# A GRU recurrence on one core: six 256-column matmuls on constant operands in each step that has no input products

## The chip, the cores and the metric

The kernel runs on one core of a Trainium2 chip. The metric is the device time of one execution in microseconds (us). TensorE (PE in the profile, PEld for its weight loads) does the matmuls, VectorE (DVE), ScalarE (ACT) and GpSimd (POOL) the element-wise work, SyncE (SP) issues DMAs. TensorE's clock has two levels here, 2.4 GHz (written 1.00 in the profile) and 1.2 GHz (0.50).

## The reference

Four layers run one after the other on x of shape (8, 256, 512), each added to its input: a masked attention over channels, a modulated attention over tokens, a GRU over the 256 tokens, and an attention over eight block sums with a layer norm. The change lies in the GRU. Cut to what matters:

```python
def cell(h, x):
    gi = x @ W_ih + b_ih
    gh = h @ W_hh + b_hh
    i_r, i_z, i_n = jnp.split(gi, 3, axis=-1)
    h_r, h_z, h_n = jnp.split(gh, 3, axis=-1)
    r = jax.nn.sigmoid(i_r + h_r)
    z = jax.nn.sigmoid(i_z + h_z)
    n = jnp.tanh(i_n + r * h_n)
    h_new = (1.0 - z) * n + z * h
    return (h_new, h_new)
x = x + scan(cell, cond, x)        # 256 steps, batch 8, width 512
```

## The kernel before, in words

The first two layers (`attention`) take the first 1137 us, the recurrence the stretch from 1139 to 2028 us, the last layer (`block_attention`) the rest.

**A step of the recurrence.** Each engine walks the same list of 256 steps, held together by semaphores. The state is kept as two float16 parts (high and low), each weight too. On TensorE, `gate` (L1252) issues matmuls of 16 columns (8 batch rows, high and low part) with a new 128x128 weight load before each; a step has 96 of them, for the gates r (into `pA`), n (`pB`) and z (`pC`). The order is written out by hand: 32 of them (16 for r, 8 for z, 8 for n) need the first half of the state alone and stand behind the first of these waits, the other 64 behind the second:

```python
pe.wait_ge(lo_done, step * 2 + 1)
...
pe.wait_ge(lo_done, step * 2 + 2)
```

Between, VectorE sums the halves (L1447, L1451), ScalarE takes sigmoid and tanh (L1356) and writes the next step's starting values into the banks (`seed`, L1347), VectorE forms the new state (L1492) and splits off its low part (L1497), which releases TensorE for the next step (`lo_done`). GpSimd adds the state to x and copies the next step's input term (L1535, once per step).

**Blocks of steps.** `blocks` (L1203) cuts the 256 steps into 8 blocks of 32. In each of the first seven, 8 plain steps come first (`begins` true), then 24 product steps, which also compute the input products for the next block: eight matmuls of 256 columns per step (`products`, L1244), issued after the step's own 96, into bank 0 of `pD`. In every second plain step of these blocks GpSimd splits x for the next block into float16 parts (`split`, L1529 and L1531). The last block has 32 plain steps, without products and without a split. So 88 steps are plain: 7 times 8, and 32.

`pG[1]`, bank 1 of `pD`, is used by the products ahead of the recurrence only. `w_in` holds the split input weights and isn't written during the recurrence.

Of the kernel before, what the change touches and what calls it, by code (L numbers as in the profile page):

```python
# [14 lines left out]
P = 128  # L15

B, N, D = 8, 256, 512
# [3 lines left out]
NC, DC = N // P, D // P  # L21
# [3 lines left out]
TB = N // NB  # L25
# [1114 lines left out]
def recurrence(nc, sem, sb, W_ih, W_hh, b_ih, b_hh, Wk3, Wo3, pA, pB, pC, pD, xT, ident, condT, rep, w_ih, woT, block_sums,  # L1140
               norm, norm_from):

    with ExitStack() as ctx:  # L1143
# [3 lines left out]
        w_in, wi_lo = [w_ih[0][:, n, :, :] for n in range(2)], w_ih[3]  # L1147
# [45 lines left out]
        pG = [pD[:, 0, 0:B * TB], pD[:, 1, 0:B * TB]]  # L1193
# [9 lines left out]
        def blocks(eng, step, split, product):  # L1203


            with eng.Fori(0, BLOCKS - 1) as blk:
                with eng.Fori(0, PLAIN // BODY) as k:
                    for j in range(BODY):
                        step(blk * TB + k * BODY + j, j, blk, True)
                        if j == 0:  # L1210
                            split(blk + 1, k)
                with eng.Fori(0, RZ) as m:
                    for j in range(BODY):
                        step(blk * TB + m * BODY + (PLAIN + j), j, blk)
                        product(blk + 1, m, j, False)
                with eng.Fori(RZ, MC) as m:
                    for j in range(BODY):
                        step(blk * TB + m * BODY + (PLAIN + j), j, blk)
                        product(blk + 1, m, j, True)
            with eng.Fori(0, TB // BODY) as k:  # L1220
                for j in range(BODY):
                    step(k * BODY + (N - TB + j), j, BLOCKS - 1, True)

        @block.sync
        def _(sp):
            sp.dma_start(bih_c[:, :], b_ih.rearrange("(c p) -> p c", p=P), allow_slow_non_contiguous=True).then_inc(b_ld, 16)
            sp.dma_start(bhh_c[:, :], b_hh.rearrange("(c p) -> p c", p=P), allow_slow_non_contiguous=True).then_inc(b_ld, 16)
            sp.dma_start(staged, W_hh.rearrange("(c p) n -> p c n", p=P)).then_inc(w_ld, 16)
            for tile, w in ((wk, Wk3), (wo, Wo3)):
                sp.dma_start(tile, w.rearrange("(c p) n -> p c n", p=P)).then_inc(wko_ld, 16)  # L1230

            *columns, gamma_bc, norm_ld = norm
            cond, rms_w, beta, gamma = norm_from
            for tile, row in zip(columns, (cond[1:2, :].rearrange("a n -> (a n)"), rms_w, beta)):
                sp.dma_start(tile[:, :], row.rearrange("(c p) -> p c", p=P), allow_slow_non_contiguous=True).then_inc(norm_ld, 16)
            sp.dma_start(gamma_bc[:, :], gamma.rearrange("(a n) -> a n", a=1).broadcast_to([P, D])).then_inc(norm_ld, 16)

        @block.tensor
        def _(pe):
            def products(m, k, bank):  # L1240

                for w in range(2):
                    for part in range(2):
                        last = nc.tensor.matmul(bank, w_in[w][:, k, bass.ts(m, P)], x_part[:, part, k, :, :].rearrange("p b t -> p (b t)"),  # L1244
                                                start=(k == 0 and w == 0 and part == 0), stop=(k == DC - 1 and w == 1 and part == 1))
                return last

            def step(step, j, blk, begins=False):

                pe.wait_ge(seeded, step * 6 + 4)  # L1250

                def gate(ps, first, part, ks):  # L1252
                    for c in CHUNKS[part]:
                        o = (c - CHUNKS[part][0]) * 2 * B
                        for k in ks:
                            for w in w_part:
                                last = nc.tensor.matmul(ps[part][:, o:o + 2 * B], w[:, k, (first + c) * P:(first + c) * P + P],  # L1257
                                                        moving[j % 2][:, k, :, :].rearrange("p s b -> p (s b)"), start=False,
                                                        stop=(k == DC - 1), skip_group_check=True)
                    return last  # L1260


                R, Z, N_ = 0, DC, 2 * DC
                K_A, K_B = CHUNKS
                pe.wait_ge(lo_done, step * 2 + 1)
                gate(pR, R, 1, K_A)
                gate(pR, R, 0, K_A)
                gate(pZ, Z, 0, K_A)
                gate(pN, N_, 0, K_A)
                pe.wait_ge(lo_done, step * 2 + 2)  # L1270
                gate(pR, R, 0, K_B).then_inc(r_ps, 1)
                gate(pZ, Z, 0, K_B).then_inc(z_ps, 1)
                gate(pN, N_, 0, K_B).then_inc(n_ps, 1)
                gate(pR, R, 1, K_B).then_inc(r_ps, 1)
                pe.wait_ge(seeded, step * 6 + 6)
                gate(pN, N_, 1, K_B)
                gate(pN, N_, 1, K_A).then_inc(n_ps, 1)
                gate(pZ, Z, 1, K_A)
                gate(pZ, Z, 1, K_B).then_inc(z_ps, 1)

            def nothing(*_):
                pass

            def product(blk, m, j, is_n):
                if j == 0:
                    pe.wait_ge(x_lo, blk * DC + DC)
                    pe.wait_ge(gi_out, blk * MC + m)
                for k in range(j * DC // BODY, (j + 1) * DC // BODY):
                    last = products(m, k, pG[0])
                if j == BODY - 1:  # L1290
                    last.then_inc(gi_ps, 1)


            def first_products(m):
                if m >= 2:
                    pe.wait_ge(gi_out, m - 1)
                for k in range(DC):
                    if m == 0:
                        pe.wait_ge(x_lo, k + 1)
                    last = products(m, k, pG[m % 2])  # L1300
                last.then_inc(gi_ps, 1)


            def transpose(n):
                w, bank = ((wk, pA), (wk, pB), (wo, pC), (wo, pA))[n]
                if n == 3:
                    pe.wait_ge(wT_ok, 1)
                for hf in range(2):
                    kc = 2 * (n % 2) + hf
                    for hc in range(DC):  # L1310
                        last = nc.tensor.transpose(bank[:, hf, hc * P:hc * P + P], w[:, kc, hc * P:hc * P + P], ident[:, :])
                last.then_inc(wT_ps, 1)

            pe.wait_ge(wi_lo, DC)
            for m in range(RZ):
                first_products(m)
            pe.wait_ge(wko_ld, 32)
            for n in range(MC - RZ):
                transpose(n)
                first_products(RZ + n)  # L1320
            pe.wait_ge(wT_ok, 4)

            pe.wait_ge(w_lo, DC)
            pe.wait_ge(lo_done, 2)
            for ps in (pR, pN, pZ):
                for part in range(2):
                    last = nc.tensor.matmul(ps[part], w_part[0][:, 0, 0:P], moving[0][:, SLICE[part], :, :].rearrange("p c s b -> p (c s b)"),
                                            start=True, stop=True)
            last.then_inc(begun, 1)
            blocks(pe, step, nothing, product)  # L1330

        @block.scalar
        def _(act):
# [38 lines left out]
            def nothing(*_):  # L1372
                pass
# [35 lines left out]
        def _(dve):  # L1409
# [108 lines left out]
            def nothing(*_):  # L1518
                pass
# [322 lines left out]
```

## Time and profile before

| | us |
|---|---|
| median of 3 runs (lowest, highest) | 2088.25 (2083.18, 2089.26) |
| the profiled execution | 2086.28 |
| span of its trace, first to last instruction | 2084.4 |
| TensorE busy | 1862.4 (89%) |
| VectorE busy | 1268.6 (61%) |
| ScalarE busy | 1117.4 (54%) |
| GpSimd busy | 376.8 (18%) |
| TensorE's mean granted clock | 0.878 |

Busy time is the time in which an engine had an instruction running. For TensorE it counts each matmul to its modelled end, so a row of 16-column matmuls that overlap shows about 0.17 us each and what a run of matmuls takes is read from the starts of its rows. "idle before" in square brackets is the time in which the engine had nothing running ahead of that row, with the instruction whose result ended the wait.

### The profile page before, as it was taken

What the parts mean: (1) busy time and instruction counts of PE and PEld (TensorE: products, weight loads), DVE (VectorE), ACT (ScalarE), POOL (GpSimd) and SP (SyncE); (2) the same over time, 40 slices, a digit from 0 to 9 for tenths busy, and PEclk for the clock granted to TensorE, in tenths of its full rate; (3) what the DMA queues carried; (4) which work ended last, traced back from release to release, by engine and by line L of the source; (5) the groups of instructions that cost most, each with busy time, mean ns of one, the idle gap of its engine ahead of it and who ended that gap; (6) DMA issues with size and microseconds to landing.
All of it is one profiled execution on the core that took longest, in us unless ns stands there. A gap on an engine that the chain in (4) does not pass through costs nothing. (4 is left out here: it accounts for less than half of the span.)

```text
span 2084.4 us, 86393 instructions
## 1 busy us (share of the span) xinstructions
PE 1862.4 (89%) x32542; PEld 1372.1 (66%) x32542; DVE 1268.6 (61%) x5543; ACT 1117.4 (54%) x4105; POOL 376.8 (18%) x1398
## 2 busy tenths in 40 slices
PE   7877998999989999999978998989898999999876
PEld 4234364454635546355557898989898989889775
DVE  6454483645736366374143777777777777777766
ACT  0342636546364463636553565656565666666554
POOL 3000000000000000000000333333334333333335
PEclk7788999999999999999998697969697988989556
DMA  5122203132041321302123000000000000000002
GB/s 190 70 66 71 68 21 106 53 76 83 9 110 42 82 78 35 95 15 74 69 61 107 1 1 0 0 0 0 0 0 0 0 0 0 0 0 0 0 0 81
DMA packets 103527, 86.76 MB, mean 42 GB/s; under 512 B 15616, under 2 KB 90496, under 8 KB 103440
## 3 DMA queue, kind: packets, MB, share of 16 engines
q1 hardware_dynamic: 101392, 84.38, 14.0%
q8 instruction: 59, 0.97, 0.2%
q10 hardware_dynamic: 1664, 1.18, 0.2%
q14 instruction: 28, 0.23, 0.0%
q0 software_dynamic: 384, 0.01, 0.0%
HBM read 60.20 MB, written 21.00 MB: 39 GB/s over the span
## 5 line engine op out<-in xcount | busy, mean ns | idle before, releaser
L1257 PE MATMUL bank_pair_A<-moving,rep 128*128 128x16 f16 x8192 | 328.4, 172 | 67.2 <-DVE moving L1497 64.1
L1257 PEld LDWEIGHTS bank_pair_A<-moving,rep 128*128 128x128 f16 x8192 | 268.4, 99 | 96.4 <-DVE moving L1497 81.2
L1257 PE MATMUL bank_pair_B<-moving,rep 128*128 128x16 f16 x8192 | 321.3, 171 | 0.0
L1257 PE MATMUL bank_pair_C<-moving,rep 128*128 128x16 f16 x8192 | 321.3, 171 | 0.0
L1356 ACT ACTIVATE r_gate<-r_pre 128x16 f32<-128x16 f32 x512 | 110.5, 216 | 305.6 <-DVE r_pre L1447 305.6
L1257 PEld LDWEIGHTS bank_pair_C<-moving,rep 128*128 128x128 f16 x8192 | 265.8, 99 | 0.0
L1257 PEld LDWEIGHTS bank_pair_B<-moving,rep 128*128 128x128 f16 x8192 | 265.8, 99 | 0.0
L1244 PE MATMUL bank_pair_D<-x_part,w_in 128*128 128x256 f16 x1536 | 211.5, 286 | 5.8 <-ACT gi_rz L1383 3.3
L1137 POOL TENSOR_TENSOR x<-x,w_in 128x512 f32<-128x512 f32 x8 | 10.2, 1274 | 962.5 <-DMA w_in<-w_in 962.5
L1447 DVE TENSOR_REDUCE r_pre<-bank_pair_A 128x16 f32<-128x32 f32 x512 | 98.1, 192 | 137.5 <-PE bank_pair_A L1257 136.4
L834 ACT ACTIVATE probs<-bank_pair_A 128x1024 f32<-128x1024 f32 x128 | 131.0, 1024 | 90.5 <-PE bank_pair_A L598 90.1
L1043 DVE TENSOR_REDUCE head_max<-bank_pair_A 128x2 f32<-128x1024 f32 x128 | 155.7, 1216 | 36.3 <-PE bank_pair_A L579 36.2
L1043 DVE TENSOR_REDUCE head_max<-bank_pair_B 128x2 f32<-128x1024 f32 x128 | 155.4, 1214 | 13.9 <-PE bank_pair_B L579 13.9
L1244 PEld LDWEIGHTS bank_pair_D<-x_part,w_in 128*128 (+1 forms) x1536 | 143.5, 101 | 26.8 <-ACT gi_rz L1383 3.5
L1535 POOL COPY n_terms<-gi_n 128x32 f32 (+1 forms) x257 | 54.3, 211 | 530.1 <-DVE moving L1497 431.9
L610 PE MATMUL bank_pair_C<-probs,w_in 128*32 128x512 f32 x1024 | 139.7, 618 | 1.0 <-ACT probs L834 0.2
L834 ACT ACTIVATE probs<-bank_pair_B 128x1024 f32<-128x1024 f32 x128 | 130.8, 1022 | 16.3 <-PE bank_pair_B L598 16.3
L1356 ACT ACTIVATE z_gate<-z_pre 128x16 f32<-128x16 f32 x512 | 110.4, 216 | 25.0
L1456 DVE TENSOR_TENSOR n_terms<-bank_pair_B,r_gate 128x32 f32<-128x32 f32 x512 | 97.7, 191 | 38.0 <-ACT r_gate L1356 0.9
L598 PEld LDWEIGHTS bank_pair_A<-rep 128*128 128x128 f16 x512 | 41.2, 98 | 114.7 <-ACT probs L834 68.4
L885 ACT ACTIVATE sq<-bank_pair_C 128x256 f32<-128x256 f32 x48 | 18.4, 384 | 174.6 <-PE bank_pair_C L640 174.6
L1451 DVE TENSOR_REDUCE z_pre<-bank_pair_C 128x16 f32<-128x32 f32 x512 | 95.8, 187 | 20.6
(260 smaller groups left out, 3639.4 us busy)
## 6 DMA issues: line engine op xcount, KB each, us to landing
rep<-parts SPq DMA_DIRECT2D x256, 64.0 KB
parts<-parts SPq DMA_DIRECT2D x48, 256.0 KB, 2.1
q_rep<-parts SPq DMA_DIRECT2D x32, 256.0 KB, 4.7
k_rep<-parts SPq DMA_DIRECT2D x64, 128.0 KB, 2.8
w_in<-in_x_dram SPq DMA_DIRECT2D x8, 512.0 KB, 4.0
x<-in_x_dram SPq DMA_DIRECT2D x8, 512.0 KB, 4.3
parts<-parts SPq DMA_DIRECT2D x32, 128.0 KB, 2.5
out_dram<-res SPq DMA_DIRECT2D x16, 256.0 KB, 2.1
```

The costliest lines, as they stand in the source:

```text
L598: last = nc.tensor.matmul(pair[u % 2][:, j // 2, (j % 2) * N:(j % 2) * N + N], k_rep[:, h, kc * P:kc * P + P], q_rep[:, h, queries], start ...
L610: last = nc.tensor.matmul(pC[32 * j:32 * j + 32, g % 2, :], v_aug[:, kc, 4 * g + j, :], probs[w % 2][:, j, :], start=(kc == 0), stop=(kc = ...
L834: nc.scalar.activation(probs[u // 2 % 2][:, :, u % 2 * N:u % 2 * N + N], pair[u % 2][:, :, :].rearrange("p a (b t) -> p (a b) t", b=2), AC ...
L885: nc.scalar.activation(sq[m % 2][:, :], qk_bank[m % 3][:, 0:N], ACT.Square).then_inc(sq_ok, 1)
L1043: nc.vector.tensor_reduce(head_max[:, 2 * n:2 * n + 2], pair[n % 2][:, :, :], AX.X, ALU.max).then_inc(s_max, 1)
L1244: last = nc.tensor.matmul(bank, w_in[w][:, k, bass.ts(m, P)], x_part[:, part, k, :, :].rearrange("p b t -> p (b t)"), start=(k == 0 and w ...
L1257: last = nc.tensor.matmul(ps[part][:, o:o + 2 * B], w[:, k, (first + c) * P:(first + c) * P + P], moving[j % 2][:, k, :, :].rearrange("p s ...
L1356: nc.scalar.activation(dst[:, SLICE[part], :], src[:, SLICE[part], :], func, scale=1.0 / GS).then_inc(done, 1)
L1447: nc.vector.tensor_reduce(r_pre[:, SLICE[part], :], halves(pR[part]), AX.X, ALU.add).then_inc(r_sum, 1)
L1451: nc.vector.tensor_reduce(z_pre[:, SLICE[part], :], halves(pZ[part]), AX.X, ALU.add).then_inc(z_sum, 1)
L1456: nc.vector.tensor_tensor(n_terms[:, SLICE[part], 0:2, :], pN[part].rearrange("p (c s b) -> p c s b", s=2, b=B), r_gate[:, SLICE[part], :] ...
L1535: nc.gpsimd.tensor_copy(n_terms[:, :, 2, :], gi_n[:, bass.ds(step, 1), :, :].rearrange("p o c b -> p (o c) b")).then_inc(n_in, 1)
```

## The change

At the end of TensorE's part of a step, if the step is plain (`begins`), six matmuls follow. Their stationary operand is a 128x128 piece of the high part of `w_in`, their moving operand 256 columns of its low part, and they write bank 1 of `pD`. Nothing reads that bank before the last layer overwrites it, they carry no semaphore and wait for none. The 168 product steps, and all other engines, stay as they are. TensorE gets 88 times 6, that is 528 matmuls more, each with its weight load.

```diff
                 gate(pN, N_, 1, K_A).then_inc(n_ps, 1)
                 gate(pZ, Z, 1, K_A)
                 gate(pZ, Z, 1, K_B).then_inc(z_ps, 1)
+                if begins:
+                    for k in range(6):
+                        nc.tensor.matmul(pG[1], w_in[0][:, k % DC, 0:P], w_in[1][:, k % DC, 0:B * TB], start=True, stop=True)
 
             def nothing(*_):
                 pass
```

## Rows read from the trace of the kernel before

**Rows 1.** The page: TensorE's granted clock in 40 slices, in tenths

```profile
PEclk7788999999999999999998697969697988989556
```

**Rows 2.** Windows, TensorE alone: stretch, length, busy (matmuls), granted clock, DMA

```profile
1142.00:1170.00 28.00, 21.66 (x750) 0.50 0.01 2
1170.30:1182.30 12.00, 12.00 (x288) 0.50 0.01 1
1183.00:1251.00 68.00, 67.81 (x2100) 1.00 0.00 1
1258.00:1282.00 24.00, 18.46 (x643) 0.50 0.00 0
1282.60:1284.60 2.00, 2.00 (x26) 0.50 0.00 0
...
1923.50:2025.00 101.50, 83.16 (x2875) 0.50 0.00 0
```

**Rows 3.** Timeline of GpSimd, L1535 alone, one per step: start, length

```profile
1172.26 0.21 POOL L1535 COPY n_terms<-gi_n 128x32 f32 x1 [1.97 <-DVE moving L1497]
...
1185.04 0.21 POOL L1535 COPY n_terms<-gi_n 128x32 f32 x1 [2.86 <-DVE moving L1497]
1188.39 0.21 POOL L1535 COPY n_terms<-gi_n 128x32 f32 x1 [1.95 <-DVE moving L1497]
...
1198.37 0.21 POOL L1535 COPY n_terms<-gi_n 128x32 f32 x1 [1.92 <-DVE moving L1497]
...
1259.79 0.21 POOL L1535 COPY n_terms<-gi_n 128x32 f32 x1 [1.06 <-DVE moving L1497]
...
1266.92 0.21 POOL L1535 COPY n_terms<-gi_n 128x32 f32 x1 [1.07 <-DVE moving L1497]
...
1990.15 0.21 POOL L1535 COPY n_terms<-gi_n 128x32 f32 x1 [2.04 <-DVE moving L1497]
...
1996.93 0.21 POOL L1535 COPY n_terms<-gi_n 128x32 f32 x1 [2.04 <-DVE moving L1497]
```

**Rows 4.** Timeline of TensorE: end of a plain step, start of the next

```profile
1253.93 0.39 PE L1257 MATMUL bank_pair_C<-moving,rep 128*128 128x16 f16 x10
1255.07 0.56 PE L1257 MATMUL bank_pair_A<-moving,rep 128*128 128x16 f16 x16 [0.74 <-DVE moving L1497]
...
1258.82 0.59 PE L1257 MATMUL bank_pair_A<-moving,rep 128*128 128x16 f16 x16 [1.04 <-DVE moving L1497]
...
1260.98 0.57 PE L1257 MATMUL bank_pair_C<-moving,rep 128*128 128x16 f16 x16
1262.17 0.59 PE L1257 MATMUL bank_pair_A<-moving,rep 128*128 128x16 f16 x16 [0.61 <-DVE moving L1497]
```

**Rows 5.** Timeline: a split on GpSimd beside VectorE's low part of the state

```profile
1265.15 0.70 POOL L1531 TENSOR_TENSOR x_part<-xT,x_part  x1 [0.18 <-POOL x_part L1529]
1265.36 0.53 DVE L1497 TENSOR_TENSOR moving<-state,moving 128x16 f16<-128x16 f32 x1
```

**Rows 6.** Timeline of TensorE: products in two product steps

```profile
1174.77 1.87 PE L1244 MATMUL bank_pair_D<-x_part,w_in 128*128 128x256 f16 x8
1176.42 0.62 PE L1257 MATMUL bank_pair_A<-moving,rep 128*128 128x16 f16 x16
...
1206.54 1.03 PE L1244 MATMUL bank_pair_D<-x_part,w_in 128*128 128x256 f16 x8
1207.41 0.55 PE L1257 MATMUL bank_pair_A<-moving,rep 128*128 128x16 f16 x16
```

**Rows 7.** Windows, TensorE alone, columns as in rows 2: the attention, a block's end

```profile
1069.70:1073.10 3.40, 1.86 (x13) 1.00 0.00 0
...
1585.10:1588.50 3.40, 3.15 (x102) 1.00 0.00 0
1588.50:1591.90 3.40, 2.78 (x96) 0.50 0.00 0
```

**Rows 8.** Timeline of TensorE: the first matmuls of the last layer

```profile
2029.19 1.09 PE L1631 MATMUL bank_pair_B<-block_sums,rep 128*128 128x64 f32 x4 [3.37 <-PEq L1143]
```

## The prediction

> **What bounds the kernel now.** I read the page first: TensorE is busy for 89% of the span, but its granted clock dips again and again from 1137 us on, where the recurrence runs [rows 1]. Then the windows cut at the block borders show what the dips follow. In every one of the seven blocks the plain steps run at 0.50, the product steps reach 1.00 after a while and stay there, and the 32 plain steps of the last block run at 0.50 throughout [rows 2]. So the clock falls where a step is only its 96 small matmuls, and comes back once the eight products are added.
>
> What does a low clock cost? Step times are the distances between GpSimd's copies, one per step [rows 3]:
> - a product step at 0.50: (1185.04 - 1172.26) / 3 = 4.26 us;
> - a product step at 1.00: (1198.37 - 1188.39) / 3 = 3.33 us;
> - a pair of plain steps at 0.50 in blocks 0 to 6, one with a split: 1266.92 - 1259.79 = 7.13 us;
> - a plain step at 0.50 in the last block: (1996.93 - 1990.15) / 2 = 3.39 us.
>
> Only the first is bound by TensorE: it goes from the products straight into the next step. A plain step is bound by the chain state, matmuls, VectorE, ScalarE, state: TensorE waits 0.61 us for VectorE before it begins [rows 4]. A pair with a split is longer, by 7.13 - 2 x 3.39 = 0.35 us, because VectorE's low part is stretched to 0.53 us until GpSimd's split beside it ends [rows 5]; that has nothing to do with TensorE.
>
> So the low clock hurts in the product steps that still run at 0.50: of the seven stretches four last about 12 us (three steps) and three about 2 us (one step); rows 2 show one of each kind. That is 4 x 3 + 3 = 15 steps at 4.26 - 3.33 = 0.93 us, 14 us in all. In the last block it costs about 0.06 us a step.
>
> **The change, part by part.** Nothing is removed or moved. TensorE gets 528 matmuls of 256 columns with their weight loads; no queue, DMA or semaphore is added. They need no data of the step, so they start as soon as the last small matmul is issued, and the question is whether they are done when the new state is there. Behind them on TensorE stands the next step's first group, for which VectorE and then all others wait.
>
> *Price of one.* The products have the same shape [rows 6]: at 1.00 (1207.41 - 1206.54) / 8 = 0.109 us, at 0.50 (1176.42 - 1174.77) / 8 = 0.206 us. Six take 0.65 us or 1.24 us.
>
> *In a step at 1.00: hidden.* A small matmul's row is 0.17 us long, so ten in 0.39 us follow each other every 0.025 us and are issued until 1254.18; the next step starts at 1255.07 [rows 4]. Six added ones would be done by 1254.83, 0.24 us before. The step then costs what the chain costs, and the product steps at 1.00 show it: 3.33 us, with eight such matmuls on board. With a split 0.35 us come on top, so a pair takes 7.0 us.
>
> *In a step at 0.50: not hidden.* Sixteen in 0.57 us are 0.027 us apart and issued until 1261.41, the next step starts at 1262.17 [rows 4]; six more end at 1262.65, 0.48 us late. The step becomes bound by TensorE like a cold product step, two matmuls shorter: 4.26 - 2 x 0.206 = 3.85 us. A pair goes from 7.13 to 7.70 us, 0.29 us a step more; a step of the last block would go from 3.39 to 3.85 us, 0.46 us more. The split's cost disappears in it, since TensorE is later than VectorE.
>
> *Which steps are at which clock?* This decides. Per step TensorE streams 96 x 16 = 1536 columns in a plain step, 3584 in a product step, and 3072 in the new plain step: between what fell and what held. The nearest rows on the side that held are in the second attention, where TensorE did twelve to thirteen 256-column matmuls in 3.4 us, about 3072 columns, and was still at 1.00 after it. On the side that fell, the border of a block: at 1585 us the last product had just been issued, small matmuls followed, and 3.4 us later the clock was at 0.50 [rows 7]. A step of the last block at 3.33 us is as dense as the attention's stretch, so I let the clock **hold in the last block**. In blocks 0 to 6 a pair takes 7.0 us, its density is 5% lower, and the steps with a split have a long wait in them; I take it that the clock **falls there after a step or two**. Once at 0.50, can the added ones raise it? Cold product steps with eight needed up to three steps; six in 3.85 us are thinner in columns than eight in 4.26 us, so no: the block stays low until its products come, which then pay as before. Block 0 enters low [rows 2] and stays so for about 7 plain steps.
>
> *The sum.* Steps at 0.50: 7 in block 0 and 5.5 in each of six blocks, 40 in all, x 0.29 = +11.6 us. Last block 31 x 0.06 = -1.9 us. The cold product steps: still about 15, 0. The last layer: TensorE stands idle for 3.37 us before it [rows 8], so a clock held to the end brings it nothing, 0; the six after the last step lie in this idle time, 0. Together +9.7 us on the profiled execution's 2086.28, so 2096. That execution lay 2.0 us below the median, so against the 2088.25 us shown the forecast is **2098 us**, 0.5% slower.
>
> The Trainium skill, page "TensorE: Matmul & The Clock Gate", section "Why this matters for your kernels", speaks of something else than density: it asks that there be no long idle gaps between bursts of matmuls, and names them as what brings the clock down. This trace doesn't bear that out here: the clock fell with no wait of TensorE longer than about 1.04 us between plain steps [rows 4]. Taken at its word, it would have the clock up in all steps before and after, and the change at nothing; read as "shorter gaps hold the clock", it is the first rival.
>
> **The rivals.**
> 1. *The clock holds in all plain steps after block 0.* For it: the gaps at 1.00 shrink to some 0.24 us, and the new step is nearer the product step than the old plain one. Against: a split step adds 0.35 us of waiting, and the border row. The time: 12 of the 15 cold product steps go, -11.2 us; six blocks with three pairs at 7.0 instead of 7.13, -2.3 us; last block -1.9 us; block 0 +2.0 us. Sum -13.4 us, 2075 us. It ends on the faster side; it decides if one split step at 1.00 doesn't bring the clock down. 15%.
> 2. *It holds in some of the seven blocks.* Each block that holds changes the sum by -1.6 us for its 5.5 steps, -0.4 us for its pairs and -1.9 us for two cold product steps, about -3.9 us; with two to four of six the total is +2 to -6 us, 2082 to 2090 us. 18%.
> 3. *It falls in the last block too.* For it: a single fall is enough, since nothing in this block raises the clock again. Its 31 steps then cost 31 x 0.46 = +14.3 us instead of -1.9 us: 2098 + 16.2 = 2114 us. Against: the attention's row, the same columns in the same time. 12%.
>
> **How the numbers follow.** The forecast has 55%, its own range 2092 to 2103 us: the number of steps before the fall moves it by 0.29 us each (35 to 45 steps), cold product steps by 0.93 us each, where a few more or fewer are likely because the blocks' borders move against the clock's changes. A measurement of this kernel tells about 0.3% (6.3 us) from no change. Slower by more: nearly all of the forecast and of rival 3, 0.64. Faster by more: rival 1 and the edge of rival 2, 0.17. Between: the rest, 0.19. The range leaves out rival 1 and the last of rival 3: 2081 to 2114 us.
>
> **What would show it right or wrong.** The granted clock of plain steps: 0.50 for most of each plain stretch in blocks 0 to 6, with GpSimd's copies 3.85 us apart; 1.00 from 1920 us on to the end of the recurrence, with copies 3.33 us apart. In the windows from the first product of a block to 1.00, still 2 to 12 us. If copies are 3.85 us apart in the last block, rival 3 is right; if the product steps of blocks 1 to 6 are all at 3.33 us, rival 1. The forecast is wrong in kind if plain steps at 0.50 stay at 3.4 to 3.7 us (the matmuls would then be cheaper than the products), or if plain steps at 1.00 are longer than 3.4 us without a split.

## The result, and the profile after

The change made the kernel slower: 2107.56 us median of 4 executions (2106.87 to 2111.59) against 2088.03 us (2083.18 to 2089.26; one execution more than in the table ahead of the prediction), a ratio of the two times of 1.0098 with a 95% interval of 1.0078 to 1.0117, or +19.5 us. The forecast was +9.7 us. The sign, the mechanism and the price of a step were right; in one place, the last block, the clock did the opposite of what the forecast let it do.

The page of the kernel after, in the lines that answer to [rows 1]:

```profile
span 2109.7 us, 87449 instructions
...
PE 1951.9 (93%) x33070; PEld 1434.9 (68%) x33070; DVE 1270.7 (60%) x5543; ACT 1119.0 (53%) x4105; POOL 376.3 (18%) x1398
...
PE   7877998999999999999978999999999999999996
...
PEclk7788999999999999999997897969697979888556
```

TensorE is busy 89.5 us longer, and its mean granted clock is 0.875, as good as the 0.878 before: the added matmuls kept it working and did not keep its clock up. In windows cut at the clock's changes (length, TensorE's busy time and matmuls, granted clock, DMA share, GB/s), the plain stretches of blocks 0, 1 and 2, a part of block 2's cold product steps, and the last block:

```profile
1147.00:1173.00 26.00, 26.00 (x697) 0.50 0.00 1
...
1262.00:1289.00 27.00, 27.00 (x725) 0.50 0.00 0
1375.00:1401.00 26.00, 26.00 (x695) 0.50 0.00 0
1405.30:1408.70 3.40, 3.40 (x78) 0.50 0.00 0
1942.00:2046.00 104.00, 104.00 (x2757) 0.50 0.00 0
```

In [rows 2] the same stretches were at 0.50 with TensorE busy for 77% to 82% of them; now it is busy all the time, still at 0.50. GpSimd's copies, one per step, in a plain stretch of block 1 and in the last block:

```profile
1268.31 0.21 POOL L1538 COPY n_terms<-gi_n 128x32 f32 x1 [2.11 <-DVE moving L1500]
1272.48 0.21 POOL L1538 COPY n_terms<-gi_n 128x32 f32 x1 [1.57 <-DVE moving L1500]
1276.00 0.21 POOL L1538 COPY n_terms<-gi_n 128x32 f32 x1 [2.11 <-DVE moving L1500]
...
1993.49 0.21 POOL L1538 COPY n_terms<-gi_n 128x32 f32 x1 [2.36 <-DVE moving L1500]
...
2001.17 0.21 POOL L1538 COPY n_terms<-gi_n 128x32 f32 x1 [2.36 <-DVE moving L1500]
```

A cold pair with a split takes 1276.00 - 1268.31 = 7.69 us (7.13 before, [rows 3]; forecast 7.70), a cold step of the last block (2001.17 - 1993.49) / 2 = 3.84 us (3.39 before; forecast 3.85). TensorE's timeline at the start of the last block shows the moment at which the clock falls, and what it costs:

```profile
1932.72 0.36 PE L1257 MATMUL bank_pair_A<-moving,rep 128*128 128x16 f16 x8
...
1934.34 0.81 PE L1282 MATMUL bank_pair_D<-w_in 128*128 128x256 f16 x6
1935.31 0.56 PE L1257 MATMUL bank_pair_A<-moving,rep 128*128 128x16 f16 x16 [0.15 <-DVE moving L1500]
1935.72 0.34 PE L1257 MATMUL bank_pair_C<-moving,rep 128*128 128x16 f16 x8
1935.92 0.34 PE L1257 MATMUL bank_pair_B<-moving,rep 128*128 128x16 f16 x8
1936.36 0.36 PE L1257 MATMUL bank_pair_A<-moving,rep 128*128 128x16 f16 x8
...
1937.57 0.56 PE L1257 MATMUL bank_pair_C<-moving,rep 128*128 128x16 f16 x16
1937.99 1.44 PE L1282 MATMUL bank_pair_D<-w_in 128*128 128x256 f16 x6
1939.22 0.62 PE L1257 MATMUL bank_pair_A<-moving,rep 128*128 128x16 f16 x16
```

The first six end at 1935.15 and leave a wait of 0.15 us: hidden, as forecast. The second six run at 0.50 and go without a wait into the next step: they push it.

Where the time is, in the profiled executions (from the copies: the first one, the distances between those that begin a block, and the rest of the span):

| us | ahead of the first copy | block 0 | blocks 1 to 6 | last block | rest |
|---|---|---|---|---|---|
| before | 1138.3 | 114.5 | 666.3 | 108.3 | 57.0 |
| after | 1143.4 | 114.5 | 675.4 | 121.7 | 54.7 |

The recurrence took 9.1 + 13.4 = 22.5 us more. The 5.1 us ahead of it are not the change's: that part ran from 1134 to 1143 us in the profiles of this study, among kernels that are the same there. The rest behind the recurrence ran from 54.5 to 57.0 us in them, so its -2.3 us is not read as the change's either.

### The profile page after: what moved, and what is told of

It is laid out like the page before. It is cut to its first block and busy times, and to the rows that moved or that the text cites. A ratio compares the mean times of both kernels' runs of the same rounds, so it can differ in the third digit from the quotient of the medians.

```text
span 2109.7 us, 87449 instructions
## 1 busy us (share of the span) xinstructions
PE 1951.9 (93%) x33070; PEld 1434.9 (68%) x33070; DVE 1270.7 (60%) x5543; ACT 1119.0 (53%) x4105; POOL 376.3 (18%) x1398
## 5 line engine op out<-in xcount | busy, mean ns | idle before, releaser
L1257 PEld LDWEIGHTS bank_pair_A<-moving,rep 128*128 128x128 f16 x8192 | 278.6, 99 | 38.6 <-DVE moving L1500 17.1
L1244 PE MATMUL bank_pair_D<-x_part,w_in 128*128 128x256 f16 x1536 | 206.9, 282 | 8.5 <-ACT gi_rz L1386 5.9
L1282 PE MATMUL bank_pair_D<-w_in 128*128 128x256 f16 x528 | 122.3, 402 | 0.0
L1359 ACT ACTIVATE cand<-n_pre 128x16 f32<-128x16 f32 x512 | 107.1, 209 | 6.6 <-DVE n_pre L1467 6.6
## 6 DMA issues: line engine op xcount, KB each, us to landing
k_rep<-parts SPq DMA_DIRECT2D x64, 128.0 KB, 2.8
parts<-parts SPq DMA_DIRECT2D x32, 128.0 KB, 2.6
```

Of the source, the lines that this page charges most:

```text
L1282: nc.tensor.matmul(pG[1], w_in[0][:, k % DC, 0:P], w_in[1][:, k % DC, 0:B * TB], start=True, stop=True)
L1359: nc.scalar.activation(dst[:, SLICE[part], :], src[:, SLICE[part], :], func, scale=1.0 / GS).then_inc(done, 1)
```

## The experiments

Theory A: the clock follows how much TensorE streams in a step, and six are too few. Theory B: matmuls that nobody waits for don't hold the clock, or its waits alone bring it down. All edits are to the changed kernel. The runs came in four series, each on another chip of the record and with its own executions of the kernel before: eight, seven, four and the last block alone (chip 6); the next four (chip 7); the three with a bridge or beside it (chip 4); the last two (chip 1). A ratio is the time over that of the kernel before in the same series.

**Eight, seven and four instead of six.**

```diff
-                    for k in range(6):
+                    for k in range(8):
```

> Eight added matmuls per plain step instead of six, as many as a product step has. Theory A (the clock follows how much TensorE streams in a step; six are a little too few, even in the 3.3 us steps of the last block): the last block holds 1.00 with steps of 3.33 us, and most plain stretches of blocks 1 to 6 do too; about 13 us faster than before, 2072 to 2080 us. Theory B (matmuls on constant operands that nobody waits for do not hold the clock, or TensorE's waits alone bring it down): the clock falls in every plain stretch as with six, plain steps take 4.26 us as cold product steps do, about 0.7 us more in each of 40 steps and 0.87 us more in each of 31, 50 to 55 us slower than before, about 2140 us.

> Seven added matmuls per plain step. Theory A: the last block holds 1.00 (steps of 3.33 us, 107 us for its 32 steps against 121.7 with six); the stretches with a split in every second step may or may not hold; 2072 to 2090 us. Theory B: cold plain steps of 4.06 us everywhere, some 40 us slower than before, about 2128 us.

> Four added matmuls per plain step. Both theories: the clock falls in every plain stretch. Cold, four take 4 x 0.206 = 0.82 us against a cold wait of about 0.76 us, so the step is 4.26 - 4 x 0.206 = 3.44 us: the last block about 0.05 us a step longer than before (+1.5 us), the pairs with a split unchanged at 7.13 us; in all within 4 us of before. This tests that the added time of six is only what does not fit into the wait.

Eight: 2074.92 us median of 8, ratio to before 0.9937 (0.9917 to 0.9956). Seven: 2072.55 us of 5, ratio 0.9930 (0.9901 to 0.9959). Four: 2088.61 us of 10, ratio 1.0015 (0.9994 to 1.0036), no difference that can be told. So in this series one matmul more per step turns the loss into a gain (a later series takes that back for seven), and the first half of theory B is out: matmuls that nobody waits for do hold the clock. Its second half, the waits, is tested below. The windows of the kernel with eight, block 1's plain stretch and then to the end of the recurrence:

```profile
1254.00:1281.00 27.00, 26.31 (x797) 1.00 0.00 0
1281.20:1291.40 10.20, 10.20 (x260) 0.50 0.00 0
1291.40:1912.70 621.30, 617.09 (x18985) 1.00 0.00 0
1912.70:1919.50 6.80, 6.80 (x153) 0.50 0.00 0
1919.50:2012.00 92.50, 92.50 (x2872) 1.00 0.00 0
```

In these windows it fell twice, both times at a border between plain and product steps, and came back within 7 to 10 us (in block 0 it was low for some microseconds too, a mean of 0.64 from 1143 to 1150 us); in the last block, where it fell in the first plain steps, the eight themselves raised it. With seven it was low through block 0 and then at 1.00 to the end:

```profile
1142.00:1182.00 40.00, 40.00 (x996) 0.50 0.00 1
...
1257.00:2013.00 756.00, 748.46 (x22998) 1.00 0.00 0
```

A block that is at 1.00 throughout takes 109.2 us instead of 111.0 on average before: no cold product steps. That is where the gain lies. With four, the pairs with a split were unchanged and the last block took 109.2 us, +0.9 for the +1.5 us expected: what fits into the wait costs next to nothing.

**What the clock follows: columns, or matmuls, or waits?**

```diff
-                    for k in range(6):
-                        nc.tensor.matmul(pG[1], w_in[0][:, k % DC, 0:P], w_in[1][:, k % DC, 0:B * TB], start=True, stop=True)
+                    for k in range(4):
+                        nc.tensor.matmul(pD[:, 1, 0:448], w_in[0][:, k % DC, 0:P], w_in[1][:, k % DC, 0:448], start=True, stop=True)
```

> Four added matmuls of 448 columns: as many columns as seven of 256 (1792), and the same time at 1.00 (0.76 us), with fewer matmuls and weight loads than the six that fell. Columns theory: as seven, the clock holds from block 1 to the end, copies 3.42 and 3.33 us apart in the last block, about 2073 us. Instruction theory (the number of matmuls or weight loads counts): it falls as with four or six, cold plain steps of 2.60 + 4 x 0.373 = 4.1 us, about 2128 us.

```diff
-                    for k in range(6):
-                        nc.tensor.matmul(pG[1], w_in[0][:, k % DC, 0:P], w_in[1][:, k % DC, 0:B * TB], start=True, stop=True)
+                    for k in range(30):
+                        nc.tensor.matmul(pG[1][:, 0:2 * B], w_in[0][:, k % DC, 0:P], w_in[1][:, k % DC, 0:2 * B], start=True, stop=True)
```

> Thirty added matmuls of 16 columns, 0.75 us at 1.00 and 0.80 us at 0.50: TensorE's wait at a plain step's end is as short as with seven of 256, but only 480 columns are streamed. Waits theory (TensorE's waits bring the clock down): holds as with seven, about 2073 us. Columns theory: falls in every plain stretch as before, and costs only what is late, about 0.05 us a cold step, 2086 to 2092 us.

One execution of each. Four of 448 columns: 2073.14 us, the clock at 1.00 where seven of 256 had it there:

```profile
1142.00:1182.00 40.00, 40.00 (x975) 0.50 0.00 1
1183.00:1253.00 70.00, 69.70 (x2149) 1.00 0.00 1
1257.00:2013.00 756.00, 748.29 (x22772) 1.00 0.00 0
```

Thirty of 16 columns: 2088.84 us, the clock at 0.50 in every plain stretch, although TensorE was busy nearly all the time (block 1, block 2, last block):

```profile
1257.00:1285.00 28.00, 27.29 (x940) 0.50 0.00 0
1370.00:1396.00 26.00, 25.27 (x889) 0.50 0.00 0
1926.00:2027.00 101.00, 100.91 (x3670) 0.50 0.00 0
```

So it is neither the number of matmuls and weight loads (four of 448 held, thirty of 16 did not) nor TensorE's waits, nor the busy share that the profile shows. What separates them is the columns streamed: four of 448 held where four of 256 had fallen, and seven of 256, the same columns in more matmuls, had held in the series before. With one execution each, these two runs don't show how often four of 448 would hold.

**The two halves of the change.** `blk` is a plain number in the last block alone, and a register in the others.

```diff
-                if begins:
+                if begins and isinstance(blk, int):
```

> The six matmuls only in the 32 steps of the last block; the plain steps of blocks 0 to 6 are as before. Both theories: the last block at 0.50 with steps of 3.84 us, +13 to +14 us against before; the rest of the change's loss (about 6 to 9 us) is gone: about 2101 us. If the loss of the last block depended on what the earlier blocks do to the clock's timing, its first steps would hold longer.

```diff
-                if begins:
+                if begins and not isinstance(blk, int):
```

> Six in the plain steps of blocks 0 to 6, none in the last block: the other half of the change. If the two halves add up, this is the change (2107.6) less the last block's 13.4 us: about 2094 us, 7 us over before. In blocks 1 to 6 the clock falls in the first plain steps as in the change, cold pairs of 7.68 us.

Last block only: 2100.14 us median of 5, ratio 1.0063 (1.0035 to 1.0091), against the 2086.65 us of before in its series +13.5 us, the last block 121.7 us. Blocks 0 to 6 only: 2093.42 us of 10, ratio 1.0024 (1.0007 to 1.0042), the last block 108.4 us and blocks 1 to 6 675.5 us, as in the change. By the ratios the halves are 0.63% and 0.24%, together 0.87%; the change is 0.98%, with an interval of 0.78% to 1.17%. They add up within it.

**Seven without the last block, and what seven is worth.**

```diff
-                if begins:
-                    for k in range(6):
+                if begins and not isinstance(blk, int):
+                    for k in range(7):
```

> Seven added matmuls in the plain steps of blocks 0 to 6, none in the last block. If the gain lies in the product steps that no longer start at 0.50, this keeps nearly all of it: the last block takes 108.3 us instead of 107.8, so about 2073 us, within 2 us of seven everywhere. If holding the clock in the last block matters too (by its steps or in the last layer), it is slower than seven everywhere by more than that.

2077.75 us median of 10, ratio 0.9954 (0.9938 to 0.9969). Its profile is that of seven everywhere up to the last block (blocks 1 to 6 655.1 against 655.3 us), which takes 108.4 us at 0.50 instead of 107.8 at 1.00. So a plain step gains next to nothing from the clock, 0.02 us; the gain is in the product steps behind it. The median is 5 us above seven's; against the before of its own series (2090.22 us) the two intervals overlap, so I don't read a difference from it.

**A bridge ahead of step 0.** With seven, block 0 stayed low (118.1 us). TensorE waits 1.35 us there for the first starting values in seven's trace. The second edit is the number of matmuls in each plain step: 7, 8 or 9 in place of 6.

```diff
             last.then_inc(begun, 1)
+            pe.wait_ge(gi_out, MC - 1)
+            for k in range(12):
+                nc.tensor.matmul(pG[0], w_in[0][:, k % DC, 0:P], w_in[1][:, k % DC, 0:B * TB], start=True, stop=True)
```

> Seven added matmuls per plain step everywhere, and twelve more of 256 columns ahead of step 0, in TensorE's wait of 1.5 us for the first step's starting values (into bank 0 of pD, once its product is out). With seven alone the clock fell there and stayed low through block 0 (118.0 us against 109.2 for the blocks at 1.00). If that wait is what let it fall, block 0 takes 109 to 110 us and the kernel is 8 us faster than with seven alone, about 2064 us, 1.1% under before. If step 0 itself (5.3 us long, waiting for its own engines) lets the clock fall, block 0 stays at 118 us and nothing is gained.

> Eight added matmuls per plain step and the same twelve ahead of step 0. Eight at 1.00 take 0.87 us and just fit into the wait, so no slower than seven where the clock holds; where it falls, eight can raise it again within a few plain steps, which seven did not (block 0: 112.6 us against 118.0). So less spread than seven with a median within 4 us of it, about 2066 us.

> Seven per plain step once more, on the same chip as the two above, to compare with them: 2072 to 2078 us, block 0 at 118 us.

Seven with the bridge: 2075.23 us median of 12, but 2071.7 to 2102.0, ratio 0.9978 (0.9946 to 1.0009). The executions stand in two groups: nine at 2071.7 to 2077.5 us with a mean granted clock of 0.951 to 0.957, three at 2094.6 to 2102.0 us with 0.913 to 0.923. The expectation fell: the clock held through step 0 and fell two steps later, and block 0 took 115.6 us.

```profile
1137.60:1147.50 9.90, 9.24 (x279) 1.00 0.01 3
1148.00:1170.00 22.00, 22.00 (x540) 0.50 0.00 0
1180.00:2012.00 832.00, 824.12 (x25353) 1.00 0.00 0
```

Seven again: 2095.99 us median of 12 (2079.6 to 2108.2) for the 2072 to 2078 us expected, ratio 1.0042 (1.0017 to 1.0066): slower than before, where the same kernel had been faster on the other chip. Its profile shows how: the last block fell, and nothing raised it.

```profile
1176.00:1908.00 732.00, 724.34 (x22337) 1.00 0.00 0
1914.00:2032.00 118.00, 118.00 (x2992) 0.50 0.00 0
```

The last block takes 128.0 us, 4.05 us a step, the price that theory B's expectation had worked out. All twelve executions have a mean granted clock of 0.904 to 0.941, where the five of the first series had 0.950 to 0.954; so it looks as if none of them held to the end. Seven is on the edge.

Block 0 took 115.8 us here, without a bridge and against 118 us expected, so the 115.6 us with the bridge are not its doing. Yet on this one chip seven took 2075 us with the bridge and 2096 us without, and the difference stands in the last block, 770 us behind the twelve matmuls. What links the two wasn't tested.

Eight with the bridge: 2072.36 us of 7 (2067.9 to 2082.4), for about 2066 us expected, ratio 0.9943 (0.9922 to 0.9964). In its profile the clock fell once, from 1830.0 to 1840.2 us; one other execution, at 2082.4 us, has a mean clock of 0.917 where the rest have 0.957 to 0.962, and no trace shows where it fell. Block 0 took 111.8 us; without the bridge it took 112.6 us on another chip, and 111.9 us in the run with eight and then six. So the bridge is worth a microsecond at most in block 0, and the eight do the rest.

**Six behind eight, and nine.**

```diff
-            with eng.Fori(0, TB // BODY) as k:
+            with eng.Fori(0, 4) as k:
                 for j in range(BODY):
                     step(k * BODY + (N - TB + j), j, BLOCKS - 1, True)
+            with eng.Fori(4, TB // BODY) as k:
+                for j in range(BODY):
+                    step(k * BODY + (N - TB + j), j, BLOCKS - 1, 6)
...
-                    for k in range(6):
+                    for k in range(8 if begins is True else begins):
```

> Eight added matmuls in all plain steps of blocks 0 to 6 and in the first 8 steps of the last block, six in its last 24. Border theory (with six the clock fell in the last block because its first plain step still waits for GpSimd and takes over 3.6 us; at the even 3.37 us behind it six are enough): the clock stays at 1.00 to the end, the last block takes 107.8 us, the kernel about 2074 us as with eight. Density theory (six per step are too few at 3.37 us as well): it falls soon after the ninth step, 22 of 24 steps at 3.84 instead of 3.37 us, +10 us, about 2085 us and a last block of 118 us.

> Nine added matmuls per plain step, with the twelve ahead of step 0. Nine at 1.00 take 0.98 us, as long as the wait or a little longer, so a plain step without a split is 3.39 us at least (96 x 0.025 + 0.98): the last block 108.5 to 109.5 us against 107.7 with eight. In return the clock should not fall at the border of the split steps and the products, as it did once with eight: 2070 to 2074 us, with less spread. If TensorE's added work delays the first group of the next step by more, the last block is above 111 us.

Eight then six: 2079.28 us median of 12 (2075.2 to 2092.6), ratio 0.9982 (0.9965 to 0.9998). The profiled execution:

```profile
1911.40:1918.20 6.80, 6.80 (x172) 0.50 0.00 0
1918.20:1938.70 20.50, 20.36 (x637) 1.00 0.01 2
1938.70:2020.00 81.30, 81.30 (x2174) 0.50 0.00 0
```

The clock fell at the border even with eight, and was raised again; then it fell in the second step with six and stayed down (last block 119.4 us; the density theory's expectation was 118). The fastest executions, 2075 us, lie where the border theory had put them, but their clock doesn't: all twelve have a mean granted clock of 0.930 to 0.942, the profiled one 0.936. Had the clock held through the last 81.3 us of that one (its span is 2082.3 us), it would be an estimated 0.955, and the eight executions with eight everywhere had 0.952 to 0.961. So six very likely fell in all twelve.

The test is not as clean as it was meant to be, though. The two loops have a border of their own, and the first step with six is a longer one, from its second group of matmuls to the next step's 1937.75 - 1934.22 = 3.53 us, where the steps with eight ahead of it took 3.33 to 3.41 us:

```profile
1934.22 0.36 PE L1260 MATMUL bank_pair_A<-moving,rep 128*128 128x16 f16 x8
...
1937.75 0.36 PE L1260 MATMUL bank_pair_A<-moving,rep 128*128 128x16 f16 x8
```

So whether six would hold if no step were longer than 3.37 us on average is still open.

Nine with the bridge: 2070.25 us median of 6 (2068.2 to 2074.9), ratio 0.9933 (0.9918 to 0.9949), within 7 us of each other, where eight with the bridge had 14 and seven 30 (with 7 and 12 executions, on another chip). In the profiled execution the clock did not fall from the first step to the last, and the mean clocks of all six lie close together, 0.959 to 0.963 (block 0 and last block):

```profile
1141.00:1250.00 109.00, 108.22 (x3331) 1.00 0.00 1
...
1909.00:2010.00 101.00, 100.91 (x3130) 1.00 0.00 0
```

The last block took 108.4 us instead of 107.7 with eight and the bridge, the price of the ninth matmul. This is the version to keep so far: 0.67% under before, and by the two ratios 1.6% under the change. Eight with the bridge is within the intervals of it, nine without a bridge wasn't run, and nine was timed in one series only.

## Why the prediction was right and wrong

**Right: the prices.** Hidden at 1.00 (a wait of 0.15 us was left), not hidden at 0.50; a cold pair 7.69 for 7.70 us, a cold step 3.84 for 3.85. In blocks 0 to 6 the clock fell in the first plain steps, as forecast.

**Near in sum, wrong in a term: "the cold product steps: still about 15, 0".** After the change there were 11 (copies about 4.2 us or more apart), -3.7 us. The plain steps cost more than 11.6 us in return: 21 cold pairs x 0.56 = 11.8, and 0.6 us at the borders, where the first product step follows a late group (3.46 for 3.37 us, seven times). That makes +8.7 us; measured was +9.1 for +11.6 us. The other kernel with six in these blocks had 12, those with none, four or thirty small ones 14 to 17, so the four may be the change's, though the two groups lie only two steps apart; why six ahead of the products should shorten the cold stretch behind them wasn't tested.

**Wrong: "hold in the last block".** This is the step that failed. The clock was at 1.00 through the first plain step and fell in the second, whose six added matmuls already ran at 0.50; nothing raised it again. The forecast rested on one row of the attention [rows 7]: thirteen 256-column matmuls in 3.4 us at 1.00, taken as equal to a step of the last block. The row was a weak likeness. Its stretch, from 1069.7 us, begins with a wait until 1070.70; from there on TensorE did sixteen such matmuls in the 3.36 us to 1074.06, 4096 columns, more than even a product step has, and only then paused:

```profile
1070.70 0.61 PE L675 MATMUL bank_pair_A<-k_rep,q_rep 128*128 128x256 f16 x4 [1.27 <-DMA k_rep<-parts]
1071.15 0.60 PE L675 MATMUL bank_pair_B<-k_rep,q_rep 128*128 128x256 f16 x4
1071.88 0.39 PE L675 MATMUL bank_pair_A<-k_rep,q_rep 128*128 128x256 f16 x2
1072.48 0.39 PE L675 MATMUL bank_pair_A<-k_rep,q_rep 128*128 128x256 f16 x2 [0.21 <-DVE head_max L1070]
1073.07 0.39 PE L675 MATMUL bank_pair_B<-k_rep,q_rep 128*128 128x256 f16 x2 [0.21 <-DVE head_max L1070]
1073.67 0.39 PE L675 MATMUL bank_pair_B<-k_rep,q_rep 128*128 128x256 f16 x2 [0.20 <-DVE head_max L1070]
```

On the other side, a step of the last block is longer than I took it for. An even one takes 3.37 us at 1.00, not 3.33, and the first plain step is not an even one: from its second group of matmuls to the next step's it takes 1936.36 - 1932.72 = 3.64 us, where the two product steps ahead of it took 3.45 and 3.34 (1925.93, 1929.38, 1932.72). The border theory of the run with eight and then six took GpSimd's late copy of the input term for the reason; the copy does wait for ScalarE to take out the last product. But the trace doesn't bear the rest out: VectorE's sum that reads the copy comes 1.23 us behind the second group in this step as in the one before (1933.95 - 1932.72, 1930.61 - 1929.38). What is late is ScalarE, which stands idle for 0.21 us with no wait that the profile shows before it writes the next starting values:

```profile
1930.61 0.21 DVE L1467 TENSOR_REDUCE n_pre<-n_terms 128x16 f32<-128x48 f32 x1
...
1933.25 0.21 POOL L1538 COPY n_terms<-gi_n 128x32 f32 x1 [2.35 <-ACT gi_n L1386]
...
1933.95 0.21 DVE L1467 TENSOR_REDUCE n_pre<-n_terms 128x16 f32<-128x48 f32 x1
...
1934.62 0.20 ACT L1350 ACTIVATE bank_pair_A<-gi_rz 128x32 f32 x1 [0.21 <-issue]
```

This step and the first with six behind eight are both the first of a new loop in the program; why they are longer is open. Which of the two, the longer first step or the 3.37 us of the even ones, brought the clock down with six is open too; seven held behind a first step of 3.65 us in its own trace.

The term was -1.9 us and measured +13.4: rival 3, which had 12% and was priced at 31 x 0.46 = 14.3 us. Its total of 2114 us was 6 us high. It stood on +25.9 us: 2.5 us too much for blocks 0 to 6 and 0.9 us too much for the last block, against the +22.5 us of the recurrence in the two profiled executions; the other 3 us lie between these and the +19.5 us of the medians, whose interval is 16.3 to 24.4 us.

**Mis-sized: what the clock is worth to a plain step.** I took 0.06 us from product steps at 1.00 (3.33 us). Steps of the last block at 1.00 took 3.37 us against 3.39 at 0.50: 107.8 for 108.3 us, 0.5 us in 32 steps. Had the clock held there, the term would still have been 1.4 us too large a gain.

**The chances.** Rivals 1 and 2 had 33%; neither shows in the six's profile. What would have been rival 1 came with seven and eight, at 2073 and 2075 us, where it had been priced at 2075: the 12 cold product steps are what it is worth.

**TensorE's waits.** The Trainium skill, page "TensorE: Matmul & The Clock Gate", section "Why this matters for your kernels", names idle gaps between bursts of matmuls as what brings the clock down. The runs speak against reading this as "shorter waits hold the clock": thirty small matmuls left TensorE 0.7 us of waiting in 28 us, and it stayed at 0.50, where eight large ones with the same wait held 1.00.

## What to carry to other kernels

Work that only keeps a clock up has to be dense enough in every step that it covers, the odd ones at the borders included: on the edge it is paid at the slow clock, where it doesn't fit into the wait any more, and the loss (here 0.45 us a step) is larger than what the clock gives. Price such work at both clocks before adding it, look for where the slow clock really costs (here in 15 product steps, not in 88 plain ones), and leave a margin of a matmul or two if the wait has room for it. A gain that rests on the edge can turn round in another series of the same kernel, so time it more than once, and compare each execution's mean granted clock: it hints at which ones held where there is no trace. A second loop that is put in to hold a step's work apart makes a border of its own; look at the step there before reading the result.

## What the runs showed of the hardware

The granted clock followed the columns streamed, not TensorE's busy share: busy for 104 of 104 us with six of 256 columns a step, or for 100.9 of 101 us with thirty of 16, it stayed at 0.50, and busy for 26.3 of 27 us with eight of 256 it stayed at 1.00. Seven gave 2072.3 to 2078.4 us in one series and 2079.6 to 2108.2 in another, with the same instructions. The two series ran on different chips (6 and 4), whose times of the kernel before are alike (2086.65 and 2086.47 us); and on chip 4 seven with the bridge held in nine of twelve executions, by their mean clock. Whether the chip, the timing of the kernel or chance is behind it is open.
